# Top-2 routing and the weight splits of an expert layer, moved from a stage of their own into the slots of the attention before it

## The reference, cut to what matters

```python
q = xt @ Wq.T                                   # layer 0, attention, 8 heads
logits = (scores * cmask + (1.0 - cmask) * NEG) * rmask
out = softmax(logits) @ q, heads joined, @ Wo.T
probs = softmax(x @ w_router)                   # layer 0, experts: x is that output
topk_w, topk_i = top_k(probs, 2)
topk_w = topk_w / sum(topk_w)
for ex in range(8):
    hid = silu(x @ w_gate[ex]) * (x @ w_up[ex])
    out = out + coef[:, ex:ex + 1] * (hid @ w_down[ex])
x = x + out
...
x = x + L1_ffn(L1_cond(x))                      # layer 1
```

## Time and profile before

| | us |
|---|---|
| median of 3 runs (2155.53 to 2160.58) | 2156.62 |
| the profiled execution: its time | 2158.13 |
| its span, first to last instruction | 2156.0 |
| PE busy | 1704.8 (79%) |
| DVE busy | 1079.7 (50%) |
| ACT busy | 619.3 (29%) |
| POOL busy | 274.1 (13%) |

### The profile page before, as it was taken

The page is one execution under the profiler, slowest core; times in us unless marked ns, Lnnn a source line. Parts: engine busy times, 40 slices in busy tenths (PEclk is TensorE's granted clock), DMA queues, the critical chain, the costliest instruction groups (busy, mean ns, idle before and its releaser), DMA issues. The chain is left out here.

```text
span 2156.0 us, 33026 instructions
## 1 busy us (share of the span) xinstructions
PE 1704.8 (79%) x10731; PEld 1011.0 (47%) x10731; DVE 1079.7 (50%) x2009; ACT 619.3 (29%) x1152; POOL 274.1 (13%) x343
## 2 busy tenths in 40 slices
PE   5788888883059999356787787795599999999998
PEld 1232323321036666132344444354477777777776
DVE  5455555543433333134455555553466665665665
ACT  0343333441332222221433434341321111111111
POOL 3111111101822222201111111000000000000000
PEclk7899999996579999756798998996699999999999
DMA  4122221102944444611111111114500000000000
GB/s 147 45 55 55 54 54 54 40 11 82 356 141 83 82 82 82 174 50 30 32 39 40 39 39 39 22 29 95 133 1 10 10 0 10 10 10 0 10 10 10
DMA packets 113345, 122.00 MB, mean 57 GB/s; under 512 B 40389, under 2 KB 79193, under 8 KB 113209
## 3 DMA queue, kind: packets, MB, share of 16 engines
q1 hardware_dynamic: 96872, 86.63, 14.2%
q0 software_dynamic: 15632, 34.30, 7.6%
q10 hardware_dynamic: 768, 0.13, 0.0%
HBM read 61.17 MB, written 29.96 MB: 42 GB/s over the span
## 5 line engine op out<-in xcount | busy, mean ns | idle before, releaser
L1770 ACT ACTIVATE d_SG<-d_bank 128x256 f32<-128x256 f32 x264 | 101.4, 384 | 380.6 <-PE d_bank L1707 301.6
L301 DVE TENSOR_REDUCE a_NM<-a_bn 128x1 f32<-128x512 f32 x256 | 163.3, 685 | 83.9 <-PE a_bn L215 80.6
L1805 DVE SCALAR_TENSOR_TENSOR d_HF<-d_bank,d_SG 128x256 f32<-128x256 f32 x264 | 112.2, 425 | 170.6 <-ACT d_SG L1770 152.3
L283 ACT ACTIVATE a_EX<-a_bt 128x512 f32<-128x512 f32 x256 | 143.9, 596 | 149.5 <-PE a_bt L234 149.1
L252 PE MATMUL a_bc<-a_EX,a_V 128*64 128x512 f32 x512 | 143.1, 638 | 0.0
L215 PE MATMUL a_bn<-a_B,a_A 97*128 97x512 f16 x256 | 99.4, 421 | 46.6 <-DVE a_NM L301 28.8
L1812 DVE TENSOR_TENSOR d_H_l<-d_HF,d_H_h 128x256 f16<-128x256 f32 x264 | 112.4, 426 | 9.0
L234 PE MATMUL a_bt<-a_A,a_B 98*128 98x512 f16 x256 | 91.7, 388 | 19.3 <-ACT a_EX L283 17.4
L301 DVE TENSOR_REDUCE c_NM<-c_bn 128x2 f32<-128x512 f32 x128 | 81.0, 681 | 44.9 <-PE c_bn L215 41.2
L864 PE MATMUL b_TX<-identh,R 128*128 128x128 f16 x312 | 24.2, 221 | 91.7 <-DVE b_wdl L1020 90.3
L215 PEld LDWEIGHTS a_bn<-a_B,a_A 97*128 97x128 f16 x256 | 22.6, 98 | 157.6 <-DVE a_NM L301 113.6
(11 more groups left out here) (346 smaller groups left out, 4013.6 us busy)
## 6 DMA issues: line engine op xcount, KB each, us to landing
R<-slot_rows SPq DMA_DIRECT2D x39, 264.0 KB, 2.7
b_stage<-in_L_ffn_w_gate SPq DMA_DIRECT2D x8, 704.0 KB, 7.4
b_stage<-in_L_ffn_w_up SPq DMA_DIRECT2D x8, 704.0 KB, 7.1
a_xb<-in_x SPq DMA_DIRECT2D x8, 512.0 KB, 3.6
a_A<-a_H SPq DMA_DIRECT2D x64, 64.0 KB, 2.9
a_B<-a_H POOLq DMA_DIRECT2D x64, 64.0 KB, 2.6
a_CT<-a_CS SPq DMA_DIRECT2D x32, 128.0 KB
b_stage<-in_L_ffn_w_down SPq DMA_DIRECT2D x8, 512.0 KB, 5.4
```

Source lines behind the costliest of these rows:

```text
L283: nc.scalar.activation(self.EX[s % 4][:, :], self.bt[s % 2][:, :], ACT.Exp).then_inc(self.exp_done, 1)
L301: self.nc.vector.tensor_reduce(self.NM[:, s * cols:(s + 1) * cols], self.bn[s % 2][:, :].rearrange("p (k n) -> p k n", k=cols), AX, ALU.ma ...
L1770: nc.scalar.activation(SG[k % 3][:, :], GU[(f + 3) % 4][:, 0:CH], ACT.Silu, scale=1.0 / WS).then_inc(silu, 1)
L1805: V.scalar_tensor_tensor(out=HF[:, :], in0=b[:, CH:2 * CH], scalar=1.0 / WS, in1=SG[k % 3][:, :], op0=ALU.mult, op1=ALU.mult).then_inc(mul ...
```

## The change

Routing and splits move into the slots of the first attention; the result is the same.

- Steps `w0`, `w1`, `w2` (DVE: low halves of expert b's three weights, slots 1, 3 and 7 of batch b) and `h0`, `h1`, `h2` (ACT: high halves for the next batch's number, slots 24, 27 and 29, and in the opening behind `shift`). Both halves go to one buffer `a_WHL`, and SP stores them to DRAM (`keep_weights`) and loads the next expert's weights (`load_weights`).
- `logit` (slot 15 now) picks the top two of 256 tokens on DVE; `exp` (slot 18) weighs them; `rank` (slot 21) ranks them within the experts with a running count `run`; POOL (`route`) makes the two coefficients of each token and scatters the 256 rows in four indirect DMAs. All this for the batch before.
- At the attention's end DVE makes the table of tiles from the counts.
- `layer0_routed` begins with SP writing the padding (8 DMAs), then the first tiles are loaded, and behind tile 3 the halves of experts 1 to 7 are read back from DRAM; those of expert 0 are read on ACT's queue.

```diff
+GU = KF * F0
+DN = 3 * T0
+W_SIZE = (GU, GU, DN)
+W_AT = (0, 2 * GU, 4 * GU)
+W_ALL = 2 * GU + DN
...
+    walk([("nat", s) for s in range(c.slots)] + [("shift",), ("h0",), ("h1",), ("h2",)], opening, b1=b0)
...
-        plan = c.plan(18, {5: ("recip",), 9: ("spread",), 11: ("rows",), 13: ("out",), 16: ("logit",), 22: ("q0",), 27: ("q1",)},
+        plan = c.plan(22, {1: ("w0",), 3: ("w1",), 5: ("recip",), 7: ("w2",), 9: ("spread",), 11: ("rows",), 13: ("out",),
+                           15: ("logit",), 18: ("exp",), 21: ("rank",), 22: ("q0",), 24: ("h0",), 27: ("q1", "h1"), 29: ("h2",)},
                       ("shift", "values"))
...
+                def load_weights(e, i):
+                    if i < 2:
+                        w = (w_gate, w_up)[i]
+                        sp.dma_start(stage[i][:, :].rearrange("p (k f) -> p k f", k=KF),
+                                     w[e].rearrange("(k p) f -> p k f", p=P)).then_inc(st_in[i], 16)
+                    else:
+                        d = stage[2][:, :].rearrange("p (k f) -> p k f", k=3)
+                        sp.dma_start(d[:, 0:2, :], w_down[e][0:2 * P, :].rearrange("(k p) f -> p k f", p=P)).then_inc(st_in[2], 16)
+                        sp.dma_start(d[0:F0 - 2 * P, 2, :], w_down[e][2 * P:F0, :]).then_inc(st_in[2], 16)
+
+                def keep_weights(e, more=True):
+
+                    for i in range(3):
+                        sp.wait_ge(w_lo, 3 * e + i + 1)
+                        for h in range(2):
+                            dst = g.half_d[bass.ds(e, 1), h] if i == 2 else g.half_gu[bass.ds(e, 1), 2 * i + h]
+                            sp.dma_start(dst.rearrange("o p f -> (o p) f"), part(h, i)).then_inc(w_kept[i], 16)
+                        if more:
+                            load_weights(e + 1, i)
+
                 a.assemble(sp, b0, a.A, a.a_in, (H, L, H))
                 a.assemble(sp, b1, a.A, a.a_in, (H, L, H))
+                sp.wait_ge(st_clear, 1)
+                for i in range(3):
+                    load_weights(0, i)
...
                         load(sp, n)
+                        keep_weights(2 * i + q)
                         a.assemble(sp, n, a.A, a.a_in, (H, L, H))
                         a.sp_context(sp, Batch(i, q))
+                keep_weights(NB - 2)
                 a.sp_context(sp, Batch(NB // 2 - 1, 0))
+                keep_weights(NB - 1, False)
                 a.sp_context(sp, Batch(NB // 2 - 1, 1))
                 sp.wait_ge(g.x_copied, 16)
+                for k in w_kept:
+                    sp.wait_ge(k, 32 * (NB + 1))
...
+                def route(n):
+
+                    chain = Chain(pool_step, HEAD_STEPS * n.idx)
+
+                    def did(ins):
+                        chain.did(ins)
+                        chain.wait(pool)
+                        pool.sem_inc(rows_begun, 1)
+
+                    head = R[:, 2 * n.par:2 * n.par + 2, :]
+                    pool.wait_ge(row_free, n.idx + 1)
+                    pool.sem_inc(rows_begun, 1)
+                    did(Q.tensor_copy(head[:, :, E:E + 1].rearrange("p t o -> p (t o)").bitcast(I32), r.token[:, :]))
+                    did(Q.tensor_scalar(r.token[:, :], r.token[:, :], float(S0), None, ALU.add))
+                    pool.wait_ge(exed, n.idx + 1)
+                    pool.sem_inc(rows_begun, 1)
+                    did(Q.tensor_tensor(r.c[:, :, :], r.oh2[:, :, :], each(r.ex[:, :]), ALU.mult))
+                    did(Q.tensor_tensor(r.c[:, :, :], r.c[:, :, :], r.oh1[:, :, :], ALU.add))
+                    did(Q.tensor_tensor(head[:, :, 0:E], r.c[:, :, :], each(r.inv[:, :]), ALU.mult))
+                    assert chain.n == HEAD_STEPS
+                    pool.sem_inc(weighed, 1)
+                    pool.wait_ge(rowed, n.idx + 1)
+                    pool.wait_ge(g.placed, n.idx + 1)
+                    pool.sem_inc(rows_begun, 1)
+                    for u in range(2):
+                        for k in range(2):
+                            Q.indirect_dma_start(out=g.slots[:, :],
+                                                 out_offset=bass.IndirectOffsetOnAxis(ap=r.place_i[:, 2 * n.par + k, u:u + 1], axis=0),
+                                                 in_=R[:, 2 * n.par + u, :], in_offset=None).then_inc(scattered, 16)
+                    if not (isinstance(n.idx, int) and n.idx == NB - 1):
+                        pool.wait_ge(scattered, 64 * (n.idx + 1))
+                        pool.sem_inc(row_free, 1)
...
+                def rank(n, uses):
+                    pe.wait_ge(chosen, n.idx + 1)
+                    bank = a.pe_take(pe, uses)
+                    MM = nc.tensor.matmul
+                    MM(bank[:, 0:2 * E], g.tri[:, :], r.MH[:, :, :].rearrange("p t e -> p (t e)"), start=True, stop=True)
+                    MM(bank[:, E:2 * E], g.ones[:, :], r.MH[:, 0, :], start=False, stop=True, skip_group_check=True)
+                    for t in range(2):
+                        mm = MM(bank[:, 2 * E:3 * E], g.ones[:, :], r.MH[:, t, :], start=(t == 0), stop=(t == 1),
+                                skip_group_check=True)
+                    mm.then_inc(a.proj_made, 1)
...
+                def weigh(n):
+                    act.wait_ge(chosen, n.idx + 1)
+                    nc.scalar.activation(r.ex[:, :], r.s[:, :], ACT.Exp).then_inc(exped, 1)
+
+                def split(n, i):
+                    act.wait_ge(st_in[i], (16, 16, 32)[i] * (n.idx + 1))
+                    act.wait_ge(w_kept[i], 32 * (n.idx + 1))
+                    nc.scalar.activation(part(0, i), stage[i][:, :], ACT.Copy, scale=WS).then_inc(w_hi, 1)
...
+                    did(V.tensor_scalar(r.l[:, :, :], bank[:, 0:2 * E].rearrange("p (t e) -> p t e", t=2), 1.0 / WS, None, ALU.mult))
+                    dve.sem_inc(a.proj_out, 1)
                     dve.sem_inc(turned_free, 1)
-                    nc.vector.tensor_scalar(g.logits[:, bass.ds(2 * n.idx, 2), :],
-                                            bank[:, 0:2 * E].rearrange("p (t e) -> p t e", t=2), 1.0 / WS, None,
-                                            ALU.mult).then_inc(a.proj_out, 1)
-
-                PRE_STEPS, POST_STEPS = 6, 0
+                    dve.wait_ge(weighed, n.idx + 1)
+                    pick(r.l[:, :, :], r.m1[:, :], r.oh1[:, :, :])
+                    did(V.scalar_tensor_tensor(out=r.l2[:, :, :], in0=r.oh1[:, :, :], scalar=-BIG, in1=r.l[:, :, :],
+                                               op0=ALU.mult, op1=ALU.add))
+                    pick(r.l2[:, :, :], r.m2[:, :], r.oh2[:, :, :])
+                    did(V.tensor_tensor(r.MH[:, :, :], r.oh1[:, :, :], r.oh2[:, :, :], ALU.add))
+                    did(V.tensor_tensor(r.s[:, :], r.m2[:, :], r.m1[:, :], ALU.subtract))
...
+                def weigh(n, chain):
+
+                    dve.wait_ge(exped, n.idx + 1)
+                    chain.did(V.tensor_scalar(r.inv[:, :], r.ex[:, :], 1.0, WS, ALU.add, ALU.mult))
+                    chain.wait(dve)
+                    V.reciprocal(r.inv[:, :], r.inv[:, :]).then_inc(exed, 1)
+
+                def rank(n, uses, chain):
+
+                    def did(ins):
+                        chain.did(ins)
+                        chain.wait(dve)
+
+                    bank = a.taken(dve, uses)
+                    if n.first:
+                        dve.wait_ge(ones_set, 15)
+                    dve.wait_ge(row_free, n.idx + 1)
+                    did(V.tensor_tensor(r.t[:, :, :], bank[:, 0:2 * E].rearrange("p (t e) -> p t e", t=2), both(g.run[:, :]), ALU.add))
+                    did(V.tensor_tensor(g.run[:, :], g.run[:, :], bank[:, 2 * E:3 * E], ALU.add))
+                    dve.sem_inc(a.proj_out, 1)
+                    did(V.tensor_tensor(r.l2[:, :, :], r.t[:, :, :], r.oh1[:, :, :], ALU.mult))
+                    did(V.tensor_reduce(r.place[:, 0, :], r.l2[:, :, :], AX, ALU.add))
+                    did(V.tensor_tensor(r.l2[:, :, :], r.t[:, :, :], r.oh2[:, :, :], ALU.mult))
+                    did(V.tensor_reduce(r.place[:, 1, :], r.l2[:, :, :], AX, ALU.add))
+                    did(V.tensor_copy(r.place_i[:, 2 * n.par:2 * n.par + 2, :], r.place[:, :, :]))
+                    dve.sem_inc(g.placed, 1)
+
+                def split(n, i):
+                    dve.wait_ge(w_hi, 3 * n.idx + i + 1)
+                    nc.vector.scalar_tensor_tensor(out=part(1, i), in0=stage[i][:, :], scalar=WS, in1=part(0, i),
+                                                   op0=ALU.mult, op1=ALU.subtract).then_inc(w_lo, 1)
...
+                dve.wait_ge(g.placed, NB)
+                did(V.tensor_copy(rt.pad_i[:, :], g.run[0:1, :]))
...
+        def load_weights(queue, e):
+            queue.dma_start(W[:, e, 0:4 * GU].rearrange("p (s f) -> p s f", s=4),
+                            g.half_gu[e].rearrange("s p f -> p s f")).then_inc(w_in[e], 16)
+            queue.dma_start(W[:, e, 4 * GU:].rearrange("p (s f) -> p s f", s=2),
```

(33 more changed lines are left out.)

344 lines of the change are left out of this document (163 added, 181 removed).

## The result

The changed kernel takes **2176.77 us**, median of 7 runs (2170.39 to 2186.0), against 2156.93 for the kernel before, on the same chip: 1.0099 times as long, 95% interval 1.0083 to 1.0116. It is slower by 20 us, where 14 less were forecast. The profiled span is 2174.8 us instead of 2156.0.

A forecast was written before the change was run, and what follows sets the result against it. PE sets the attention's pace; the hole behind it is what the change dissolves. Hole -71, opening +18, loop +22, experts +17 sum to -14: median 2143 us from 2156.6, range 2122 to 2165.

The forecast's parts named there:

- The loop: Attention's loop: added steps cost 3.1 us in each of 7 batches, +22 us, bounds 11 and 61.
- ACT waits for the pick at slot 18, while PE stands still anyway: Attention's loop: ACT's wait for the pick coincides with PE's stand, which was priced at +2.0 us.
- With the chain DVE is free at 320.5: Attention's loop: the pick's DVE chain delays a maximum, so PE goes on at 321.2 to 321.5 instead of 319.4, +2.0.
- The bound of 8.7 a batch: Attention's loop, upper bound: 22 steps at 0.3 us, `w2` and PE's share with nothing covered, 61 us.
- `w2` ... about +0.3: Attention's loop: `w2`, 1.75 us on DVE between the reciprocal and the normalisation, costs about +0.3.
- The third rival: Attention's late slots: DVE becomes the bound, a batch pays up to 8.7 us, total 2182; chance 0.13.
- The hole: Last logits to first tile: PE begins at 543 instead of 613.8, -71 us, bounds -75 and -67.
- The barrier took from 515.38 ... to 515.66: Attention's end, in the hole: the barrier lasts from the end of the logits' instruction at 515.38 to 515.66.
- The experts: Experts' stage: PE stands 14 us before tile 4, then 3 us for low clock, +17 us, bounds 0 and 28.
- tile 4 lands at about 586: Experts' stage: tile 4's load waits behind 15.6 MB of weights, while PE wants it at 572.
- the order on the queue: Experts' stage: tile 4, behind the weights on SP's queue, can't pass them, so PE stands 14 us.
- The opening: Attention's opening: ACT's roundings delay the first exponential to 83.2, PE stands 23 us, +18 us net, between +14 and +22.

The follow-up runs named there:

- the pick alone: The kernel without routing in the loop, with the pick's 13 further DVE steps put back; first to seventh reciprocal 360.1 us, against 329.8 without routing.
- the kernel with late scatters: The changed kernel with the last batch's four scatters issued at the beginning of the next block; 2175.28 us, ratio 1.0082.
- the kernel with 283: The changed kernel with the pick in 7 steps on DVE instead of 14; 2150.08 us, ratio 0.9966.

## Why the prediction was wrong

**The loop (+22 forecast, +44.5 measured) is where it failed.** The step is "ACT waits for the pick at slot 18, while PE stands still anyway" and "With the chain DVE is free at 320.5 ... and PE goes on at 321.2 to 321.5 instead of 319.4: +2.0". The 2.0 us of standing are right (2.20 in the row, in each of the six turns; 2.0 a batch by the difference with the pick alone). What the step leaves out is that PE works at 0.50 of full clock behind it, 3.1 us more a batch by PE's own busy time. In the opening I had charged for that; in the loop I counted waits alone. The second thing it leaves out is the jump back: two times 3.3 us, 1.1 a batch. `rank` and `exp`, forecast at 0.8 together, are 1.3 to 2.1. The bound of 8.7 a batch was sound, the measured 7.4 lies under it. `w0`, `w1`, the roundings and "`w2` ... about +0.3" were no part of the loss: with all of them and no routing R1 to R7 is 5.4 us below before. The forecast also counted "each of the 7 batches that have the next one beside their post steps", but only six have it: beside the last batch's slots there is no `nat` step, and from the seventh reciprocal on nothing was lost. With six its +22 would have been 19, farther still from what was measured.

**The third rival came true in its size, not by its mechanism.** It decides "from 6.1 us a batch on", and 7.4 were paid; but DVE did not fall behind for all late slots. It was busy 242.8 of 379.4 us, and PE's longer waits stand behind `pick`, at the jump and behind `rank`.

**The hole (-71 forecast, -59.9 measured)** failed at "The barrier took from 515.38 ... to 515.66". That was read from an end of a block at which POOL had been idle for 110 us. With POOL at work until the end it is 9.8 us in the changed kernel to the first load, 10.8 to the first padding. All else in this term held within 1 us: pick and rank 5.2, scatters until 586.2, eight paddings in 9.7.

**The experts (+17 forecast, +22.5 measured):** the mechanism "tile 4 lands at about 586" behind the weights was right in what is seen (18.5 us of standing instead of 14, and a low clock behind), the size nearly. But the order on the queue was the wrong thing to name as the cause: another order costs the same, and on another queue the waits for tiles are as long. What binds is that a tile's buffer is loaded when the fourth add before it has landed, without slack, so that whatever slows a tile's load or an add is paid by PE. Taken away, the weights cost 2.4 us.

**The opening (+18 forecast, +15.6 measured)** was right, PE's stand of 23 us within 0.4.

Of the 34 us between forecast and result 22.5 are the loop's, 11 the boundary's, 5.5 the experts'; the opening gave 2.4 back and layer 1 some 4. That makes 33; the last one is that the profiled execution before lay 1.2 above its median. **Open stays** what the 9.8 us at the block's end are due to: they follow POOL's last instruction, scatter or multiplication (9.7 in the kernel with late scatters), but why was not tried; and which activity of PE makes the clock fall at one stand of 2.2 us and not at another. How the 1.3 to 2.1 us of rank and exponential split was not tried either.

## What to carry to other kernels

Price a wait put into a loop that keeps TensorE busy twice over: once for the stand itself, and once for the work at half clock behind it, which here was the larger part (3.1 against 2.0 us a batch). Two shorter waits in place of the long one gave 12.9 us back here. Before moving bytes beside a stage, look at its ring of buffers: if a load is issued by the release of the buffer that it needs, just in time, the stage has no room for any other traffic. Four more buffers were worth 16.5 us here, and both other orders tried with four buffers nothing or less. An engine that issues loads ahead of its own work delays that work too. And take the price of a block's end from one at which the same engine finishes last.

## What was not expected of the hardware

- With 311 listed instructions on DVE in the loop's body (waits and semaphores not listed) the jump back costs DVE 3.2 to 3.5 us, at both jumps; with 283, 277 and 225 no such wait is seen. 28 semaphore increments more in the kernel with 283 bring it back (6.5 us in two) and cost 6.7 us in all. Why the number counts was not tried.
- TensorE's granted clock was 1.00 from 352.0 to 355.2, where PE worked 1.06 of 3.2 us and then stood for 2.20, 0.79 in the next 2.2 us and 0.50 in the 2.0 after these, though PE worked again; four products took 0.9 us more there.
- The next block's first load came 9.7 to 9.8 us behind GpSimd's last instruction in ten kernels, and 0.3 us behind VectorE's in the four in which GpSimd had by then been idle for 33 to 35 us. In the changed kernel no DMA engine moved anything from 588 on until 596.
- Beside one expert's weights (2.2 MB) in flight on another queue a tile's load of 264 KB landed in 6.4 to 8.3 us instead of 2.5 to 2.9, and PE waited 1.9 to 4.3 us for it, six times.
